# Decoder layer on one core: partition sums on TensorE, all queries in the fold stage, folded values beside the first softmax, another order of VectorE and GpSimd in the cross-attention

## The chip, the cores and the metric

One core of a Trainium2 chip runs the kernel. The metric is the device time of one execution in microseconds (us), the median of the runs. Engines are named as the profile names them: PE (TensorE matmul), PEld (its weight loads), DVE (VectorE), ACT (ScalarE), POOL (GpSimd), SP (SyncE, here only DMA issues). A tile is 128 rows of the 2048 x 256 activations; there are 16.

## The reference, cut to what matters

```python
x = x + self_attention(layernorm(x)) @ wo              # 16 heads of 16, causal by pages of 64
# cross-attention, one head of width 1024, 1601 keys, context c = ctx_1024
xn = layernorm(x)
e  = (xn @ Wq.T + bq) @ (c @ Wk.T + bk).T / sqrt(1024)
e  = where(mask == 0, -2**15, e)
x  = x + softmax(e) @ (c @ Wv.T + bv) @ Wo.T + bo
# feed: ternary weight, one scale for the whole tensor
xn = (x - mean(x)) * rsqrt(var(x) + 1e-3) * ln_gamma + ln_beta     # x is first layernormed too
beta = mean(abs(weight));  w_q = clip(round(weight / (beta + 1e-5)), -1, 1)
gamma = max(abs(xn))                                   # over all rows and columns
x = x + (clip(xn * 128 / gamma, ...) @ w_q) * (gamma * beta / 128)
```

Two of these lines sum or compare over all 128 partitions: `beta` and `gamma`.

## The kernel before

Four stages run one after the other, each in `nc.Block`s whose end all engines wait for.

`self_attention` (to 553.4 us of the span) isn't touched by the change. It leaves its result in the SBUF tile `attn`.

`fold` (553.4 to 620.5 us) does two things at once. It multiplies `attn` by `wo` and adds it to `x`, normalises the sum to `xn`, turns it with PE transposes and keeps it as `x2_t` (256 features on partitions, 2048 rows). And it folds the weights of the cross-attention: `w_qk` = Wq.T Wk, `w_vo` = Wv.T Wo, a bias `bias_c`, and the values of all 1601 keys with the output weight in them, `v_out`. PE takes its steps from the list `ORDER` (lines 889 to 892) written out by hand; ACT follows the same list. In it `turn` transposes four tiles of `attn` (first copied to `attn_s` by POOL, `stage`, line 913), `output` is the product with `wo`, `norm` transposes `xn`, and `job` n is one product of weights: 0 and 1 rows of bias, 2 and 3 `w_qk`, 4 and 5 `w_vo`, 6 the bias column (32 matmuls that are one column wide, lines 1065 to 1069), 7 to 13 `v_out` for two key tiles each. DVE runs `add` and `norm` for each block of four tiles and last computes the ternary feed weight; for its mean POOL sums `abs_sum` over the partitions (`partition_all_reduce`, line 937).

`cross` (620.7 to 882.3 us) goes over the 16 tiles in program order on every engine, as a loop of pairs of tiles (`pairs`, line 1189). PE's `body(i)` first runs `score(i + 1)`: it makes q~ of the next tile (8 matmuls of 128 columns, line 1353), waits until ACT has copied it with its bias (line 1314), and multiplies it with the 1601 context columns into four PSUM banks (line 1361). Then it transposes the softmax of tile i (line 1376) and multiplies it with `v_out` (line 1388). DVE's `body(i)` copies two of the four chunks of the transposes (line 1278), then `take(i + 1)`: masked copy out of PSUM (line 1264), row maximum (line 1266). ACT computes the exponential (line 1319). POOL fills `e` with the value of masked keys for the next tile (line 1223). After the product of tile i, DVE adds it to `x`, takes mean and variance (lines 1287 to 1296), waits for seven small steps of POOL that give the scale (lines 1229 to 1241), writes `z` (line 1299), waits for POOL's products with gamma and beta (lines 1245, 1247) and takes the row maximum (line 1302), all before it touches the chunks of tile i + 1. After the loop `x3` is transposed into `x3_t`.

`feed` (882.3 us to the end) reduces the 16 row maxima, has POOL take the maximum over partitions (line 1455), and then scales, clips, multiplies with the ternary weight and stores.

Of the kernel before, what the change touches and what calls it, by code (L numbers as in the profile page):

```python
# [17 lines left out]
I32 = mybir.dt.int32  # L18
# [6 lines left out]
P = 128  # L25
# [788 lines left out]
def fold(nc, ctx, io, keep, psum):  # L814
# [7 lines left out]
    def sem(name):  # L822
# [10 lines left out]
    w_vo = sb("w_vo", [P, EC, E])  # L833
# [4 lines left out]
    abs_all = sb("abs_all", [P, 1])  # L838
    limit = sb("limit", [P, 2])
    above = sb("above", [P, EC, E])  # L840
    attn_s = sb("attn_s", [P, TPB, E])
# [14 lines left out]
    w_bank = [banks(psum, 6), banks(psum, 7)]  # L856

# [3 lines left out]
    staged = sem("staged")  # L861
# [20 lines left out]
    abs_everywhere = sem("abs_everywhere")  # L882
    limit_done = sem("limit_done")
# [3 lines left out]
    V_FIRST = 7  # L887
# [6 lines left out]
    def v_tiles(n):  # L894
        return range(2 * (n - V_FIRST), min(2 * (n - V_FIRST) + 2, S2_TILES))

    def keys_of(j):
        return P if j < S2_TILES - 1 else S2_TAIL

    with nc.Block() as block:  # L900

        @block.sync
        def _(sp):
            sp.dma_start(b_o[:, :], bass.AP(io["bo"].tensor, 0, [[0, P], [1, E]])).then_inc(b_o_loaded, 16)
            sp.dma_start(ffn_w[:, :, :], io["ffn_w"].rearrange("(c p) e -> p c e", p=P)).then_inc(ffn_w_loaded, 16)

        @block.gpsimd
        def _(pool):
            nc.gpsimd.memset(eps[:, :], LN_EPS).then_inc(set_done, 1)
            nc.gpsimd.memset(minus_half[:, :], -0.5).then_inc(set_done, 1)  # L910
            pool.wait_ge(set_done, 2)

            def stage(tb):

                pool.wait_ge(a_ready, tb * EC)
                nc.gpsimd.tensor_copy(attn_s[:, :, :], attn[:, bass.ds(tb * TPB, TPB), :]).then_inc(staged, 1)
# [13 lines left out]
            stage(0)  # L930
            with pool.Fori(0, NB - 1) as tb:
                stage(tb + 1)
                norm(tb)
            norm(NB - 1)

            pool.wait_ge(abs_ready, 1)
            nc.gpsimd.partition_all_reduce(abs_all[:, :], abs_sum[:, :], P, ReduceOp.add).then_inc(abs_everywhere, 1)

        @block.vector
        def _(dve):  # L940
# [36 lines left out]

            dve.wait_ge(w_ready, 1)
# [8 lines left out]
            with dve.Fori(1, NB) as tb:  # L987
# [3 lines left out]
            dve.wait_ge(ffn_w_loaded, 16)  # L991
            nc.vector.tensor_reduce(abs_sum[:, :], ffn_w[:, :, :], axis=mybir.AxisListType.XY, op=ALU.add,
                                    apply_absolute_value=True).then_inc(abs_ready, 1)
            dve.wait_ge(abs_everywhere, 1)
            nc.vector.tensor_scalar(keep["beta"][:, :], abs_all[:, :], 1.0 / (E * E), None, ALU.mult).then_inc(limit_done, 1)
# [10 lines left out]
        def _(act):  # L1006
            def take(n):

                act.wait_ge(w_ready, n + 1)
                bank = w_bank[n % 2]  # L1010
                if n < V_FIRST:
                    dst = {2: w_qk[:, 0, :], 3: w_qk[:, 1, :], 4: w_vo[:, 0, :], 5: w_vo[:, 1, :],
                           6: bias_c[:, :]}[n]
                    last = nc.scalar.activation(dst, bank[:, 0:EC if n == 6 else E], ACT.Copy)
                else:
                    for m, j in enumerate(v_tiles(n)):
                        rows = keys_of(j)
                        last = nc.scalar.activation(v_out[0:rows, j, :], bank[0:rows, m * E:(m + 1) * E], ACT.Copy)
                last.then_inc(w_copied, 1)
# [8 lines left out]
            def turn_norm(tb):  # L1028
                for c in range(EC):
                    act.wait_ge(n_ready, tb * EC + c + 1)  # L1030
                    nc.scalar.activation(x2_t[:, c, tb, :], n_bank[c], ACT.Copy).then_inc(n_copied, 1)

            steps = {"turn": turn_attn, "norm": turn_norm, "job": lambda n: take(n) if n >= 2 else None,
                     "output": lambda tb: None}
# [4 lines left out]
        def _(pe):  # L1039
# [5 lines left out]
            def job(n):  # L1045
# [19 lines left out]
                elif n == 6:  # L1065
# [4 lines left out]
                else:  # L1070

                    pe.wait_ge(w_copied, 4)
                    for m, j in enumerate(v_tiles(n)):
                        rows = keys_of(j)
                        last = product(bank[0:rows, m * E:(m + 1) * E], lambda e: ctx_t[:, e, j * P:j * P + rows],
                                       lambda e: w_vo[:, e, :], EC)
                last.then_inc(w_ready, 1)

            def turn(tb):

                pe.wait_ge(staged, tb + 1)
                pe.wait_ge(a_copied, tb * EC)
                for c in range(EC):
                    for k in range(TPB):
                        last = nc.tensor.transpose(a_bank[c][:, k * P:(k + 1) * P], attn_s[:, k, c * P:(c + 1) * P],
                                                   ident[:, :])
# [13 lines left out]
            def normed(tb):  # L1100
                pe.wait_ge(xn_ready, tb * TPB + TPB)
                pe.wait_ge(n_copied, tb * EC)
# [6 lines left out]
            steps = {"turn": turn, "output": output, "norm": normed, "job": job}  # L1109
# [6 lines left out]
def cross(nc, ctx, io, keep, psum):  # L1116
# [7 lines left out]
    ctx_t, w_qk, bias_c, v_out = keep["ctx_t"], keep["w_qk"], keep["bias_c"], keep["v_out"]  # L1124
    x2_t, row_fill, x3, abs_max = keep["x2_t"], keep["row_fill"], keep["x3"], keep["abs_max"]
    x3_t = keep["x3_t"]
    mask = sb("mask", [P, 2, S2], I32)
# [7 lines left out]
    gamma = sb("gamma", [P, E])  # L1135
    beta = sb("beta_row", [P, E])
# [16 lines left out]
    q_bank = psum[:, 4 * BLK - E:4 * BLK]  # L1153
    t_bank = [banks(psum, n) for n in (4, 5, 7)]
    y_bank = banks(psum, 6)

    x_bank = [[banks(psum, n) for n in pair] for pair in ((0, 1), (2, 3), (4, 5), (0, 1))]

    mask_loaded = [sem(f"mask_loaded{n}") for n in range(2)]
# [455 lines left out]
```

## Time and profile before

| what | value |
|---|---|
| time, median of 3 runs | 914.88 us (911.33 to 915.14) |
| the profiled execution: its own time, its span | 913.99 us, 912.2 us |
| PE busy | 808.8 us, 89% of the span |
| DVE busy | 581.9 us, 64% |
| ACT busy | 413.7 us, 45% |
| POOL busy | 178.3 us, 20% |
| mean granted clock of TensorE | 0.933 of full |
| PE in `cross`, products with the context (L1361) | 256 records, 95.7 us |
| PE in `cross`, products with the values (L1388) | 416 records, 94.6 us |

The span runs from the first to the last instruction; the execution's own time has 1.8 us more around it. An fp32 matmul leaves two records in the trace, so 16 records of L1361 are the 8 matmuls of one tile. The clock has two levels, 2.4 GHz (1.00) and 1.2 GHz (0.50); a window's figure between them is a mix. Idle time is shown with what ended it, in brackets.

### The profile page before, as it was taken

To read this page: it belongs to the slowest core of one execution; us is meant where nothing else is said; L and a number is where in the kernel's file an instruction comes from. 1 tells how busy PE (TensorE), PEld (TensorE's weight loads), DVE (VectorE), ACT (ScalarE), POOL (GpSimd) and SP (SyncE) were. 2 spreads that over 40 slices of the span, in tenths; PEclk is the share of its full clock that TensorE was granted. 3 is DMA by queue.
4 is the path that set the end of the run, shared out by engine and by line. 5 is a ranking of instruction groups with operands and counts; after the bars stand their busy time and mean duration, and the time that the engine had idled before them with its cause. 6 is when DMAs were issued, how large, how long until landed. Compare 5 with 4: busy or idle time off the path is not lost. (4 is left out here: it accounts for less than half of the span.)

```text
span 912.2 us, 14049 instructions
## 1 busy us (share of the span) xinstructions
PE 808.8 (89%) x4252; PEld 406.5 (45%) x4252; DVE 581.9 (64%) x1047; ACT 413.7 (45%) x851; POOL 178.3 (20%) x263
## 2 busy tenths in 40 slices
PE   7865898999899999899999798895899999999847
PEld 5431232333223332223333226783576767667636
DVE  4998497889788899888886401772244535445414
ACT  1551553766467766567777692221222222222211
POOL 2662000000000000000000000433044453534410
PEclk9995897999899999989999898998899999999977
DMA  7794311200000000000700000002112112121002
GB/s 200 206 273 126 93 48 36 59 24 24 1 1 1 0 1 1 1 1 21 249 0 1 1 1 18 1 1 86 71 36 72 62 46 72 36 72 36 1 1 92
DMA packets 27084, 47.26 MB, mean 52 GB/s; under 512 B 6048, under 2 KB 22944, under 8 KB 26272
## 3 DMA queue, kind: packets, MB, share of 16 engines
q1 hardware_dynamic: 24096, 43.81, 15.8%
q10 hardware_dynamic: 2944, 2.89, 1.2%
q8 instruction: 25, 0.41, 0.2%
q14 instruction: 19, 0.16, 0.1%
HBM read 38.16 MB, written 8.39 MB: 51 GB/s over the span
## 5 line engine op out<-in xcount | busy, mean ns | idle before, releaser
L507 DVE TENSOR_REDUCE part_max<-psum 128x1 f32<-128x512 f32 (+3 forms) x560 | 344.2, 670 | 72.6 <-PE psum L706 68.0
L619 ACT ACTIVATE probs<-psum 128x512 f32<-128x512 f32 (+3 forms) x640 | 295.4, 539 | 170.8 <-PE psum L731 157.7
L706 PE MATMUL psum<-k_stack,q_stack 96*128 (+6 forms) x640 | 221.2, 374 | 17.9 <-DVE psum L493 11.5
L731 PE MATMUL psum<-q_stack,k_stack 98*128 98x512 bf16 (+6 forms) x640 | 209.2, 366 | 19.6 <-DMA q_stack<-shift 12.5
L746 PE MATMUL psum<-probs,v_group 128*17 128x512 f32 (+3 forms) x1280 | 151.0, 545 | 0.3
L706 PEld LDWEIGHTS psum<-k_stack,q_stack 96*128 (+3 forms) x640 | 61.1, 100 | 172.3 <-DVE part_max L507 81.5
L731 PEld LDWEIGHTS psum<-q_stack,k_stack 98*128 98x128 bf16 (+3 forms) x640 | 61.5, 100 | 109.9 <-issue 37.9
L1361 PE MATMUL psum<-q_stack,qc_t 128*128 128x512 f32 (+1 forms) x256 | 95.7, 528 | 12.8 <-ACT qc_t L1314 12.8
L407 POOL COPY v_group<-v_all 128x272 f32 (+1 forms) x40 | 16.8, 425 | 429.9 <-PE psum L746 429.9
L1388 PE MATMUL psum<-v_out,p_t 128*128 128x256 f32 (+1 forms) x416 | 94.6, 385 | 3.1 <-DVE p_t L1278 3.1
L1388 PEld LDWEIGHTS psum<-v_out,p_t 128*128 128x128 f32 (+1 forms) x416 | 79.0, 193 | 13.7 <-DVE p_t L1278 3.5
L1361 PEld LDWEIGHTS psum<-q_stack,qc_t 128*128 128x128 f32 x256 | 45.9, 194 | 63.5 <-issue 47.6
L1330 ACT ACTIVATE p_t<-psum 128x512 f32<-128x512 f32 x32 | 19.1, 598 | 103.1 <-PE psum L1376 103.1
L1319 ACT ACTIVATE e<-e,neg 128x1601 f32<-128x1601 f32 x16 | 26.1, 1632 | 79.3 <-DVE neg L1268 75.1
L746 PEld LDWEIGHTS psum<-probs,v_group 128*17 128x17 f32 x1280 | 21.5, 96 | 50.5 <-ACT probs L619 30.8
L1264 DVE COPY_PREDICATED e<-mask,psum 128x1601 f32<-128x1601 int32 x16 | 31.2, 1949 | 19.4 <-POOL e L1250 14.9
L1223 POOL TENSOR_TENSOR e<-zeros_s,row_fill 128x1601 f32<-128x1601 f32 x15 | 42.8, 2852 | 0.5 <-POOL e L1250 0.3
L1299 DVE TENSOR_SCALAR z<-x_sb,mv,scale 128x256 f32 (+1 forms) x16 | 6.6, 413 | 42.2 <-POOL scale L1241 42.2
L1278 DVE COPY p_t<-psum 128x512 f32<-128x512 f32 (+1 forms) x32 | 14.2, 484 | 29.0 <-PE psum L1376 29.0
L1266 DVE TENSOR_REDUCE neg<-e 128x1 f32<-128x1601 f32 x16 | 29.1, 1821 | 0.5
L530 DVE RECIPROCAL rsum<-psum 128x16 f32<-128x16 f32 x16 | 4.1, 254 | 37.7 <-PE psum L717 37.1
L1229 POOL TENSOR_TENSOR va<-mv,consts 128x1 f32<-128x1 f32 x16 | 3.0, 189 | 126.1 <-DVE mv L1296 126.1
(121 smaller groups left out, 708.4 us busy)
## 6 DMA issues: line engine op xcount, KB each, us to landing
mask<-in_mask SPq DMA_DIRECT2D x16, 800.5 KB, 4.4
pieces<-k_stack SPq DMA_DIRECT2D x24, 256.0 KB, 4.8
q_stack<-pieces SPq DMA_DIRECT2D x24, 256.0 KB, 4.3
k_stack<-pieces SPq DMA_DIRECT2D x24, 256.0 KB, 4.7
x_sb<-in_x SPq DMA_DIRECT2D x4, 512.0 KB, 8.7
out<-y SPq DMA_DIRECT2D x4, 512.0 KB, 2.9
q_stack<-in_ctxT SPq DMA_DIRECT2D x1, 1601.0 KB, 10.9
probs<-in_cos ACTq DMA_DIRECT2D x4, 256.0 KB
```

What stands on the lines that cost most here:

```text
L507: nc.vector.tensor_reduce(part_max[:, h:h + m, r, c:c + 1], src, axis=AX_X, op=ALU.max).then_inc(m_read, 1)
L619: nc.scalar.activation(probs[:, s % 2, h, col:BLK], s_bank[h][:, col:BLK], ACT.Exp, scale=ATTN_SCALE).then_inc(exp_done, 1)
L706: last = nc.tensor.matmul(out, q_stack[b][0:rows, g * G + h, r * P:(r + 1) * P], k_stack[c][0:rows, g * G + h, 0:keys], start=True, stop=True)
L731: nc.tensor.matmul(s_bank[h][:, col:BLK], k_stack[s // TPB][0:rows, g * G + h, (s % TPB) * P:(s % TPB + 1) * P], q_stack[b][0:rows, g * G ...
L746: last = nc.tensor.matmul(o_bank[32 * h:32 * h + VW, col:BLK], v_group[:, s, h, :], probs[:, s % 2, h, col:BLK], start=s == 0, stop=s == s ...
L1223: nc.gpsimd.tensor_tensor(e[:, 1 - h, :], zeros[:, :], row_fill[:, bass.ds(i + 1, 1)].to_broadcast([P, S2]), ALU.add).then_inc(filled, 1)
L1264: nc.vector.copy_predicated(e[:, h, :], mask[:, h, :], e_bank).then_inc(e_taken, 1)
L1266: nc.vector.tensor_reduce(neg[:, h:h + 1], e[:, h, :], axis=AX_X, op=ALU.max).then_inc(max_done, 1)
L1319: nc.scalar.activation(e[:, h, :], e[:, h, :], ACT.Exp, scale=X_SCALE, bias=neg[:, h:h + 1], accum_out=esum[:, h:h + 1]).then_inc(exp_done, 1)
L1330: nc.scalar.activation(p_t[:, j:j + m, :].rearrange("p j q -> p (j q)"), t_bank[n % 3][:, 0:m * P], ACT.Copy).then_inc(t_copied_a, 1)
L1361: last = nc.tensor.matmul(e_bank[:, c0:c1], qc_t[:, h, k, :], ctx_t[:, k, c0:c1], start=k == 0, stop=k == EC - 1)
L1388: mm = nc.tensor.matmul(y_bank[:, 0:E], p_t[0:keys, j, :], v_out[0:keys, j, :], start=j == 0, stop=j == S2_TILES - 1)
```

## The change

- `fold`, attention: `attn_s` and POOL's `stage` go; PE transposes `attn` itself.
- `fold`, queries: a step `("query", tb)` for each block of four tiles multiplies `x2_t` by `w_qk` (4 matmuls of 512 columns) and ACT writes the result with its bias back over `x2_t`. `score` in `cross` loses its 8 matmuls and the wait for ACT; ACT's `prepare` becomes one copy from SBUF, made two tiles ahead.
- `fold`, values: jobs 7 to 13 go. `cross` runs them as `V_JOBS` between `score(0)` and the first `body`, with ACT's copies before and after the first exponential.
- Partition sums: the sum of `abs_sum` is a matmul with a tile of ones (step `("sum", 0)`). In `feed` a PE transpose, a DVE maximum of one row and a matmul with ones take the place of POOL's instruction. DVE reduces the feed weight at the start of `fold`.
- Loads of gamma, beta and the first two mask tiles are issued in `fold` instead of at the start of `cross`.
- Order in `cross`: DVE's `z` and row maximum of tile i - 1 are done in `body(i)`, on both sides of `take(i + 1)`, instead of at the end of `body(i - 1)`. POOL does the fill of tile i + 1, then `finish(i - 1)`, then the seven steps of tile i (`measure`). The first pair of tiles is written out ahead of the loop.

```diff
-    JOBS = V_FIRST + -(-S2_TILES // 2)
     ORDER = [("turn", 0), ("job", 0), ("output", 0), ("job", 1), ("turn", 1), ("job", 2), ("output", 1),
              ("norm", 0), ("turn", 2), ("job", 3), ("output", 2), ("norm", 1), ("turn", 3), ("job", 4),
-             ("output", 3), ("norm", 2), ("job", 5), ("job", 6), ("job", 7), ("norm", 3)]
-    ORDER += [("job", n) for n in range(V_FIRST + 1, JOBS)]
+             ("output", 3), ("norm", 2), ("job", 5), ("job", 6), ("query", 0), ("query", 1), ("sum", 0),
+             ("query", 2), ("norm", 3), ("query", 3)]
...
+            def query(tb):
+
+                act.wait_ge(n_ready, in_n.index(("query", tb)) * EC + EC)
+                act.wait_ge(w_copied, 5)
+                for c in range(EC):
+                    nc.scalar.activation(x2_t[:, c, tb, :], n_bank[c], ACT.Identity,
+                                         bias=bias_c[:, c:c + 1]).then_inc(n_copied, 1)
...
+            def query(tb):
+
+                pe.wait_ge(n_copied, in_n.index(("query", tb)) * EC)
+                pe.wait_ge(w_copied, 2)
+                for c in range(EC):
+                    for k in range(EC):
+                        last = nc.tensor.matmul(n_bank[c], w_qk[:, k, c * P:(c + 1) * P], x2_t[:, k, tb, :],
+                                                start=k == 0, stop=k == EC - 1)
+                    last.then_inc(n_ready, 1)
...
+                nc.tensor.matmul(sum_at, ones[:, :], abs_sum[:, :], start=True, stop=True).then_inc(abs_everywhere, 1)
...
                 for n, (j, m) in enumerate(CHUNKS):
...
+                first = isinstance(i, int) and i == 0
+                if not first:
+                    scale_row(i - 1)
                 if not last:
                     take(i + 1, 1 - h)
+                if not first:
+                    largest(i - 1)
...
+            for n, tiles in enumerate(V_JOBS):
+                act.wait_ge(v_ready, n + 1)
+                for m, j in enumerate(tiles):
+                    rows = keys_of(j)
+                    last = nc.scalar.activation(v_out[0:rows, j, :], v_bank[n % 2][0:rows, m * E:(m + 1) * E], ACT.Copy)
+                last.then_inc(v_copied, 1)
+                if n == 1:
+                    exponential(0, 0)
...
             def score(i, h):
 
-                pe.wait_ge(qc_copied, i * EC)
                 pe.wait_ge(e_taken, i)
-                for c in range(EC):
-                    for k in range(EC):
-                        last = nc.tensor.matmul(q_bank[:, c * P:(c + 1) * P], w_qk[:, k, c * P:(c + 1) * P],
-                                                x2_t[:, k, :, :].rearrange("p b t -> p (b t)")[:, bass.ds(i * P, P)],
-                                                start=k == 0, stop=k == EC - 1)
-                last.then_inc(qc_ready, 1)
-                pe.wait_ge(qc_copied, (i + 1) * EC)
+                pe.wait_ge(qc_copied, i + 1)
...
             score(0, 0)
+            for n, tiles in enumerate(V_JOBS):
+
+                if n >= 2:
+                    pe.wait_ge(v_copied, n - 1)
...
+            pe.wait_ge(v_copied, len(V_JOBS))
             pairs(pe, body)
...
-            pool.wait_ge(top_done, 1)
-            nc.gpsimd.partition_all_reduce(top_all[:, :], top[:, :], P, ReduceOp.max).then_inc(top_everywhere, 1)
...
+            pe.wait_ge(top_done, 1)
+            nc.tensor.transpose(top_row, top[:, :], ident[:, :]).then_inc(top_turned, 1)
+            pe.wait_ge(top_found, 1)
+            nc.tensor.matmul(top_all, ones[0:1, :], top_1[:, :], start=True, stop=True).then_inc(top_everywhere, 1)
```

## Rows read from the trace of the kernel before

**Rows 1.** Windows: stretch, length, busy PE, PEld, DVE, ACT, POOL, PEclk, DMA, GB/s.

```profile
760.24:847.24 87.00, 82.71 (x379) 60.07 (x379) 40.84 (x67) 21.25 (x36) 37.82 (x60) 1.00 0.14 47
607.00:608.00 1.00, 1.00 (x4) 0.82 (x3) 0.26 (x1) 0.00 (x0) 0.71 (x1) 0.50 0.00 0
```

**Rows 2.** Timeline of one tile in `cross`: start, duration, engine, line, operation, idle before.

```profile
745.74 5.81 PE L1361 MATMUL psum<-q_stack,qc_t 128*128 128x512 f32 x16 [0.71 <-ACT qc_t L1314]
...
752.46 0.89 DVE L1278 COPY p_t<-psum 128x512 f32<-128x512 f32 x2 [1.23 <-PE psum L1376]
...
752.84 5.79 PE L1388 MATMUL psum<-v_out,p_t 128*128 128x256 f32 x26
...
753.66 1.95 DVE L1264 COPY_PREDICATED e<-mask,psum 128x1601 f32<-128x1601 int32 x1 [0.31 <-POOL e L1223]
...
757.68 1.63 ACT L1319 ACTIVATE e<-e,neg 128x1601 f32<-128x1601 f32 x1 [4.19 <-DVE neg L1268]
...
758.47 1.05 PE L1353 MATMUL psum<-x_t,w_qk 128*128 x8
...
760.24 4.99 PE L1361 MATMUL psum<-q_stack,qc_t 128*128 128x512 f32 x11 [0.71 <-ACT qc_t L1314]
...
762.76 0.19 POOL L1241 TENSOR_TENSOR scale<-ra,rb 128x1 f32<-128x1 f32 x1
```

**Rows 3.** Timeline of `fold`, 555 to 621 us.

```profile
555.71 1.97 PE L1085 MATMUL psum<-ident,attn_s 128*128 128x128 f32 x8 [2.46 <-POOL attn_s L916]
...
557.47 5.74 PE L1042 MATMUL psum<-q_stack 128*128 128x257 f32 x16
...
578.29 1.02 DVE L969 CUSTOM_DVE_ANT_0 dump<-xn,row_w 128x256 f32<-128x256 f32 x1
...
579.47 0.48 DVE L969 CUSTOM_DVE_ANT_0 dump<-xn,row_w 128x256 f32<-128x256 f32 x1
...
590.35 1.09 PE L1085 MATMUL psum<-ident,attn_s 128*128 128x128 f32 x8 [2.38 <-POOL attn_s L916]
...
598.19 1.04 PE L1105 MATMUL psum<-ident,xn 128*128 128x128 f32 x8
...
599.07 7.09 PE L1042 MATMUL psum<-q_stack 128*128 128x256 f32 x48
...
606.02 3.66 PE L1042 MATMUL psum<-w_vo,q_stack 128*128 128x256 f32 x8
...
610.26 1.10 ACT L1031 ACTIVATE x_t<-psum 128x512 f32<-128x512 f32 x2
...
620.09 0.38 ACT L1018 ACTIVATE v_out<-psum 65x256 f32<-65x256 f32 x1 [0.20 <-PE psum L1042]
```

**Rows 4.** Timeline of the start of `cross`.

```profile
622.77 5.81 PE L1361 MATMUL psum<-q_stack,qc_t 128*128 128x512 f32 x16 [0.71 <-ACT qc_t L1314]
...
632.23 2.84 POOL L1250 TENSOR_TENSOR e<-zeros_s,row_fill 128x1601 f32<-128x1601 f32 x1 [9.95 <-issue]
...
639.21 1.63 ACT L1319 ACTIVATE e<-e,neg 128x1601 f32<-128x1601 f32 x1 [16.49 <-DVE neg L1268]
...
641.50 8.55 PE L1361 MATMUL psum<-q_stack,qc_t 128*128 128x512 f32 x16 [2.04 <-ACT qc_t L1314]
```

**Rows 5.** Timeline of the last tile and of the start of `feed`.

```profile
867.53 5.84 PE L1388 MATMUL psum<-v_out,p_t 128*128 128x256 f32 x18 [3.09 <-DVE p_t L1278]
...
882.58 0.17 DVE L1459 TENSOR_REDUCE top<-abs_max 128x1 f32<-128x16 f32 x1 [2.52 <-PEq L1197]
888.50 0.38 POOL L1455 PARTITION_ALL_REDUCE top_all<-top  x1 [8.88 <-issue]
888.91 0.16 DVE L1462 RECIPROCAL to_q<-top_all 128x1 f32<-128x1 f32 x1 [6.16 <-POOL top_all L1455]
```

**Rows 6.** Timeline of a small PE transpose between two DVE operations in self-attention.

```profile
515.05 0.22 DVE L512 TENSOR_REDUCE neg_max<-part_max 128x16 f32<-128x64 f32 x1
...
515.72 0.28 DVE L518 CAST shift<-psum 16x128 bf16<-16x128 f32 x1 [0.45 <-PE psum L712]
```

More of the change, by code:

```diff
@@ L905, in _ @@
             sp.dma_start(ffn_w[:, :, :], io["ffn_w"].rearrange("(c p) e -> p c e", p=P)).then_inc(ffn_w_loaded, 16)
+            masks = io["mask"].rearrange("(t p) s -> t p s", p=P)
+            for name in ("gamma", "beta"):
+                sp.dma_start(keep[name + "_row"][:, :], bass.AP(io[name].tensor, 0, [[0, P], [1, E]]))\
+                    .then_inc(keep["rows_loaded"], 16)
+            for h in range(2):
+                sp.dma_start(keep["mask"][:, h, :], masks[h]).then_inc(keep["mask_loaded"][h], 16)
         @block.gpsimd
@@ L1010, in take @@
                 bank = w_bank[n % 2]
[L1011 to L1018, printed above, removed]
+                dst = {2: w_qk[:, 0, :], 3: w_qk[:, 1, :], 4: w_vo[:, 0, :], 5: w_vo[:, 1, :], 6: bias_c[:, :]}[n]
+                last = nc.scalar.activation(dst, bank[:, 0:EC if n == 6 else E], ACT.Copy)
                 last.then_inc(w_copied, 1)
@@ L1029, in turn_norm @@
                 for c in range(EC):
[L1030 removed]
+                    act.wait_ge(n_ready, in_n.index(("norm", tb)) * EC + c + 1)
                     nc.scalar.activation(x2_t[:, c, tb, :], n_bank[c], ACT.Copy).then_inc(n_copied, 1)
[L1033 to L1034 removed]
+            def query(tb):
[4 more added lines that the diff above has]
+                                         bias=bias_c[:, c:c + 1]).then_inc(n_copied, 1)
+            steps = {"turn": turn_attn, "norm": turn_norm, "query": query,
+                     "job": lambda n: take(n) if n >= 2 else None,
+                     "output": lambda tb: None, "sum": lambda n: None}
             for what, n in ORDER:
@@ L1187, in cross, with keys_of, pairs @@
     PAIRS = TILES // 2
-    def pairs(engine, body, first=None):
-        with engine.Fori(0, PAIRS - 1) as k:
+    def keys_of(j):
+        return P if j < S2_TILES - 1 else S2_TAIL
+    def pairs(engine, body):
+        for h in range(2):
+            body(h, h, False)
+        with engine.Fori(1, PAIRS - 1) as k:
             for h in range(2):
@@ L1335, in body @@
                     exponential(i + 1, 1 - h)
-            prepare(0, 0)
-            exponential(0, 0)
+            for h in range(2):
+                src = queries[:, :, 0, h * P:(h + 1) * P]
+                nc.scalar.activation(qc_t[:, h, :, :], src, ACT.Copy).then_inc(qc_copied, 1)
+            for n, tiles in enumerate(V_JOBS):
[6 more added lines that the diff above has]
+                    exponential(0, 0)
             pairs(act, body)
@@ L1392, in _ @@
             score(0, 0)
+            for n, tiles in enumerate(V_JOBS):
+                if n >= 2:
+                    pe.wait_ge(v_copied, n - 1)
+                for m, j in enumerate(tiles):
+                    for k in range(EC):
+                        last = nc.tensor.matmul(v_bank[n % 2][0:keys_of(j), m * E:(m + 1) * E],
+                                                ctx_t[:, k, j * P:j * P + keys_of(j)], w_vo[:, k, :],
+                                                start=k == 0, stop=k == EC - 1)
+                last.then_inc(v_ready, 1)
+            pe.wait_ge(v_copied, len(V_JOBS))
             pairs(pe, body)
@@ L1544, in build @@
             keep["w_qk"] = sbo("w_qk", [P, EC, E])
+            keep["w_vo"] = sbo("w_vo", [P, EC, E])
+            keep["ones"] = sbo("ones", [P, P])
+            keep["mask"] = sbo("mask", [P, 2, S2], I32)
+            keep["gamma_row"] = sbo("gamma_row", [P, E])
+            keep["beta_row"] = sbo("beta_row", [P, E])
+            keep["mask_loaded"] = [own.enter_context(nc.semaphore(f"mask_loaded{n}")) for n in range(2)]
+            keep["rows_loaded"] = own.enter_context(nc.semaphore("rows_loaded"))
             keep["bias_c"] = sbo("bias_c", [P, EC])
```

146 lines of the change are left out of this document (73 added, 73 removed).

## The prediction

> **What bounds the kernel now.** I read the busy time by windows first. Over six tiles of `cross` PE is busy for 82.71 of 87.00 us at the full clock, DVE for 40.84 and POOL for 37.82 [rows 1]: PE sets the pace and the others have half their time free. The timeline of one tile then shows where PE's other time is. A tile lasts 14.50 us (760.24 - 745.74). It is the product with the context (5.64 us to the first transpose, 5.81 with its tail), the transposes (1.46), the product with the values (5.63 to the next step), q~ of the next tile (1.05) and a wait of 0.71 for ACT's copy of q~ [rows 2]. So 1.05 + 0.72 = 1.77 us of each tile are q~ and its round trip. Third, the timeline of `fold`: DVE's norm chain sets the time up to the last block, and then PE's seven value jobs run to its end at 620.47 us [rows 3]. Fourth, the start and the end of `cross`, where PE stands still: 13 us between the first and the second product with the context, the second then at half the clock [rows 4], 3.09 us in the last tile, and the wait for POOL's maximum over partitions [rows 5].
>
> **q~ out of the loop.** `score` 2 to 15 each lose 1.77 us, if nothing else ends later than PE: 14 x 1.77 = **-24.8 us**. What is late next? Counted from the start of a product with the context, DVE's chunk copies end at +7.6 us (752.46 + 0.89 - 745.74). Then comes `z` of the tile before, moved there, which is half the size of one of the two copies that take 0.89, so 0.45 at most; 0.31 of idle stand in that place now. The masked copy then ends at about +10.1, where it ended at +9.87 (753.66 + 1.95 - 745.74). The banks are needed at +12.73, so 2.6 us are free. The exponential, which starts 4.02 us after the masked copy and takes 1.63, ends near +13.9 with its read-out, and the transposes that want it start at 12.73 + 5.64 = +18.4: 4.5 us free [rows 2]. ACT's copy of q~ is made two tiles ahead and waits for nothing late. POOL's scale of the tile before ends 4.5 us after the product with the values (762.95 - 758.47). The fill of 2.84 follows at once and ends near +7.4, before DVE's +8.1 [rows 2, 4]; that is the narrowest of these margins, and missing it by 1 us still costs PE nothing, because of the 2.6. Behind DVE's wait for the scale in `scale_row` stands `take`; behind POOL's wait for `z` in `finish` stand the seven steps, whose input comes only at the end of the tile. New period 12.73 us.
>
> **Queries in `fold`.** Four steps of 4 x 512 = 2048 columns. The 3202 columns of a product with the context take 5.64 us [rows 2], so a query takes 5.64 x 2048 / 3202 = 3.6 us. ACT copies both halves only after both are made (1.10 us by the copies of the same shape [rows 3], 1.3 with the two hand-overs), and the next query waits for that. The list runs: `norm` 2, jobs 5 and 6, query 0, 1, 2, `norm` 3, query 3. Before, the transposes of `norm` 2 start at 598.19 and job 6 ends at 606.06 [rows 3]. Two things shift this. First, PE needn't wait 2.46 us for POOL's copy of `attn`: it can start about 1.1 us earlier, as soon as the stage begins, but 1.97 us for 8 transposes and 5.74 us for job 0 (7.09 for three times the records later) are at the half clock, while later 8 transposes take 1.09 [rows 3]. Some of the gain is given back, as the clock rises no earlier for it: -0.6, bounds 0 and -3. Second, without POOL's copies one of DVE's four dot products per block takes 0.48 instead of 1.02 us [rows 3]: 2 x 0.54 = -1.1, bounds 0 and -1.1. So job 6 ends at 604.3. Query 0 is then at risk: the 3.66 us of the value job right behind job 6 cover 8 records, and the clock was 0.50 although PE was busy the whole time [rows 1, 3]. Job 6 is 32 matmuls of one column. Half that cost, +0.9, is in the sum; its bounds are 0 and +3.6. Then 3 x (3.6 + 1.3) = 14.7, the transposes and their copy 1.8, and 3.6 + 1.3 = 4.9. End of `fold`: 604.3 + 0.9 + 14.7 + 1.8 + 4.9 = 626.6, against 620.47: **+6.1 us**. The end is now a chain of hand-overs between PE and ACT; nothing covers it.
>
> **Values in the first tile.** ACT needs 0.4 us for the first copy of q~ (0.38 for 256 columns at 620.09 [rows 3]), so the first product with the context starts about 0.8 us after the stage's end and ends at +6.5. POOL's fill follows its memsets: it no longer waits 9.95 us [rows 4], since the loads are issued 70 us earlier and no `partition_all_reduce` stands before it, and ends near +5.3. From the masked copy to the end of the exponential are 4.02 + 1.63 us and 0.2 of read-out [rows 2]: done near +12.5. Meanwhile PE does 26 matmuls of 256 columns, 2 x 5.63 = 11.3 us by the product with the values [rows 2]. Every second job's bank is free in time, since the exponential holds ACT for 1.8 us only, and with the last copy the first `body` begins at +18.1. That is 626.6 + 18.1 = 644.7. The second product with the context started at 641.50 before, but took 8.55 us at the half clock against 5.81 [rows 4]; now PE was busy just before. Ends: 650.4 against 649.9, so **+0.5 us** in all to this point, the +6.1 included. The cover works both ways: 13 us of standing still take up the value jobs and the longer `fold`.
>
> **Last tile.** DVE no longer stands in the chain of `z` and POOL's products when the last transposes are ready. The product with the values keeps neither its wait of 3.09 us nor the half clock behind it: 5.84 us for 18 records, where 26 take 5.79 [rows 2, 5]. That is 3.09 + 5.84 - 18/26 x 5.79 = 4.9 us. The exponential is about 0.2 later: **-4.7 us**. The norm of tile 15 behind it is the same chain as before.
>
> **Maximum over partitions.** From the end of DVE's `top` (882.75) to `to_q` (888.91) are 6.16 us, of which POOL's instruction is 0.38 [rows 5]. Instead: PE transpose, DVE maximum, PE matmul. A DVE to PE to DVE trip takes 0.45 us [rows 6]; twice that and 0.2 for the maximum are 1.1. **-5.1 us**, bounds -3 (the trips at twice the price and more) and -5.3. The Trainium skill speaks against this edit: "GPSIMD Engine Reference", section "Engine selection", names GpSimd for reductions over partitions. The same page, "Instruction dispatch", says that the first call of freshly loaded code pays about 6 us. By the first rule alone POOL should keep the maximum and the sum would have no such term; the row sides with the second: 5.66 us without work in front of 0.38. In `fold` the sum over partitions had cover and has it now: 0.
>
> **Nothing** for the moved loads (SP issues two before them as before, and no one waits for the masks until 70 us later), the DVE reduction at the head of `fold` (512 columns, while DVE waits for the 5.74 us of job 0 [rows 3]), and the written-out first pair.
>
> **Sum.** -24.8 + 0.5 - 4.7 - 5.1 = -34.1 us. Against the profiled execution: 913.99 - 34.1 = 879.9. That run stands 0.9 below the median of 914.88, well inside the spread; I take 880.
>
> **Rivals.** (1) *PE no longer sets the pace.* DVE's `z` and POOL's fill fall on each other, or another wait takes the place of the 0.72. Then 14 x 0.72 = 10 come back: 890. For: the fill has 0.7 us of margin. Against: the banks have 2.6 us behind it. (2) *The queries run at the half clock throughout*: 4 x 3.6 more, 894. For: a drop stands behind job 6 [rows 1], and bursts of 3.6 us with gaps of 1.3 us follow. Against: after a gap of 2.38 us in `fold` 8 transposes take 1.09 us, at the full clock [rows 3]. The skill's "TensorE: Matmul & The Clock Gate", section on oscillation, describes such a loss from short gaps between groups of matmuls, and would have it in every query. (3) *POOL's wait at the start of `cross` stays* (the profile names nothing that ended it, so it may be code loading that comes anyway). With 6 us of it left, the exponential and the ACT copies behind it come 5 us later: 885. (4) *Slower than before*: in `cross` the clock falls to half and stays there, since PE has no other limit now. A tile is then 12.73 us longer, and from 34.1 / 12.73 = 2.7 such tiles on the change loses; with four it is 931. For: the half clock follows every standstill in rows 4 and 5. Against: 87 us at 1.00 with less PE work per time. (5) *Better*: the clock stays up at the start of `fold` and behind job 6 and rises sooner in `feed`: -6, so 874. (6) *The removal doesn't remove*: POOL's share of the 6.16 us was hidden. Excluded, as DVE waits for it by name [rows 5].
>
> **How the numbers follow.** Forecast 0.65, (1) 0.10, (2) 0.06, (3) 0.07, (4) 0.03, (5) 0.09. The forecast's own bounds: the start of `fold` -3, query clock -0.9 to +2.7, trips +2: 875 to 885. The range 872 to 890 takes in (1), (3) and (5) and leaves out (2), (4) and tails. A measurement of this kernel can tell about 0.5% (4.6 us) from no change. Only (4) is slower, and nothing likely lies within 0.5%: faster 0.96, same 0.01, slower 0.03.
>
> **What would show it.** The products with the context start 12.7 us apart. `fold` ends near 626 and its four queries are 4.9 us apart. The second product with the context takes 5.8 us. The last product with the values has no wait in its middle. `top` to `to_q` takes about 1.3 us. It is wrong if the period is above 13 us, or if half-clock windows stand in `cross` after its first tile.

## The result

| | before | changed |
|---|---|---|
| time, median | 913.22 us (4 runs) | 876.18 us (875.08 to 882.21, 4 runs) |
| ratio, 95% interval | | 0.9607 (0.9563 to 0.9651) |
| profiled execution: its own time, span | 913.99, 912.2 us | 882.21, 880.4 us |

By the ratio the time falls by 36 us; forecast was 880 us with a range of 872 to 890. Timed again beside three variants (control, below) the changed kernel had 877.55 us, ratio 0.9623 (0.9599 to 0.9648). The profiled execution is the longest of its runs. To see why, and to compare experiments closer than their times allow, I cut each trace at six marks: the first POOL memset of `fold`, that of `cross`, the first transpose of the softmax, the last addition to `x`, `top`, `to_q`. This table is worked out from the timelines of one execution each:

```
us             before fold  fold  first tile  other tiles  x3  top to to_q  rest   span
before              554.4   66.3     29.1       223.6      9.1     6.3      23.3   912.2
changed             556.4   72.1     25.4       192.5      9.1     1.6      23.3   880.4
control             554.3   72.1     23.8       192.5      9.1     1.6      23.8   877.0
feed_only           557.5   66.4     29.2       223.6      9.1     1.6      23.9   911.2
order_only          552.9   66.3     29.1       218.8      8.3     6.4      22.6   904.2
q_in_loop           551.7   58.0     30.3       218.8      8.2     1.6      23.5   892.1
v_in_fold           552.9   80.7     15.9       192.5      9.0     1.6      22.4   875.1
stage_back          553.0   75.7     23.8       192.5      9.1     1.6      23.7   879.3
reduce_back         553.9   72.0     31.6       192.5      8.2     1.6      23.6   883.5
mixed_jobs          554.3   72.1     23.8       192.5      9.1     1.6      23.8   877.0
more_banks          551.1   66.3     23.8       192.5      9.1     1.6      23.3   867.6
more_banks_again    554.0   66.3     23.8       192.5      8.2     1.6      23.6   870.0
both                551.2   64.6     25.5       192.5      9.0     1.6      23.2   867.7
split               549.2   72.7     15.1       192.5      8.7     1.6      22.8   862.6
```

("control" is the changed kernel once more; the other names are those of the experiments below.) The self-attention ahead of `fold` is the same code in all of them and lasts 549.2 to 557.5 us. That is nearly all of the scatter between these executions. The later stages of the same code repeat to 0.1 us except where the clock differs: "x3" is 9.1 or 8.2 us long and "rest" varies by 1.4, with the place of the half clock that starts in "x3" in every trace. The profiled changed execution has 2.0 us more in self-attention than that of before. The stages from `fold` on are 33.8 us shorter: +5.7 in `fold`, -3.7 in the first tile, -31.1 in the others, -4.7 at the maximum.

**The profile after.** Two lines of the page, the costliest PE groups of `cross` (line, engine, operation, count, busy time, mean, idle before):

```profile
L1385 PE MATMUL psum<-q_stack,qc_t 128*128 128x512 f32 (+1 forms) x256 | 93.2, 517 | 2.6 <-ACT qc_t L1361 2.1
...
L1412 PE MATMUL psum<-v_out,p_t 128*128 128x256 f32 (+1 forms) x416 | 92.7, 380 | 0.0
```

The idle time before the products with the context is 2.6 us, where it was 12.8, all of it spent on ACT's copy of q~ (page of before, the same group on line 1361). A tile of the changed kernel (start, duration, engine, line, operation), to be held against [rows 2]; of the last group only the part before the end of the window is counted:

```profile
686.34 5.71 PE L1385 MATMUL psum<-q_stack,qc_t 128*128 128x512 f32 x16
...
690.64 0.19 POOL L1235 TENSOR_TENSOR scale<-ra,rb 128x1 f32<-128x1 f32 x1
690.78 2.85 POOL L1253 TENSOR_TENSOR e<-zeros_s,row_fill 128x1601 f32<-128x1601 f32 x1
...
693.77 0.40 DVE L1287 TENSOR_SCALAR z<-x_sb,mv,scale 128x256 f32 x1
694.09 1.96 DVE L1276 COPY_PREDICATED e<-mask,psum 128x1601 f32<-128x1601 int32 x1
...
698.13 1.63 ACT L1341 ACTIVATE e<-e,neg 128x1601 f32<-128x1601 f32 x1 [4.13 <-DVE neg L1280]
...
698.97 1.45 PE L1385 MATMUL psum<-q_stack,qc_t 128*128 128x512 f32 x3
```

PE starts the next product with the context after 12.63 us, with no wait in front. The masked copy ends 9.71 us after the tile's start (forecast 10.1) and POOL's fill at +7.29 (forecast 7.4), 0.46 before the masked copy that needs it begins, where the forecast had 0.7.

`fold` and the first tile, against [rows 3, 4]:

```profile
556.42 1.06 PE L1068 MATMUL psum<-ident,attn 128*128 128x128 f32 x8 [1.20 <-PEq L285]
...
557.32 3.64 PE L1033 MATMUL psum<-q_stack 128*128 128x257 f32 x16
...
603.43 6.38 PE L1098 MATMUL psum<-x_t,w_qk 128*128 128x512 f32 x8
...
611.16 3.70 PE L1098 MATMUL psum<-x_t,w_qk 128*128 128x512 f32 x8 [1.36 <-ACT x_t L1020]
...
629.01 7.48 PE L1385 MATMUL psum<-q_stack,qc_t 128*128 128x512 f32 x16 [2.15 <-ACT qc_t L1361]
...
636.33 11.44 PE L1423 MATMUL psum<-w_vo,q_stack 128*128 128x256 f32 x52
636.74 1.96 DVE L1276 COPY_PREDICATED e<-mask,psum 128x1601 f32<-128x1601 int32 x1 [19.67 <-PE psum L1385]
...
648.24 5.81 PE L1385 MATMUL psum<-q_stack,qc_t 128*128 128x512 f32 x16 [0.47 <-ACT v_out L1366]
```

Three things in it: the stage begins at the full clock (1.06 us for the 8 transposes that took 1.97), the first query takes 6.38 us where the others take 3.70, and the first product with the context takes 7.48 where the next takes 5.81. Job 6 stands right before the first query. It is 16 matmuls of one column (8 for each of two columns), which leave 32 records; the text on the kernel before and the prediction count the records as matmuls. The clock in the windows over job 6 and the first query (stretch, length, busy PE, PEld, DVE, ACT, POOL, PEclk, DMA share, GB/s):

```profile
602.00:603.50 1.50, 1.50 (x10) 1.50 (x9) 0.89 (x6) 0.00 (x0) 0.27 (x2) 0.51 0.00 0
603.50:609.80 6.30, 6.30 (x9) 2.37 (x8) 4.88 (x11) 0.17 (x1) 3.29 (x2) 0.57 0.00 0
609.80:611.20 1.40, 0.04 (x2) 0.04 (x1) 0.40 (x3) 1.27 (x2) 0.00 (x0) 1.00 0.00 0
```

The last tile and the maximum, against [rows 5]:

```profile
838.96 1.73 PE L1400 MATMUL psum<-ident,e 128*128 128x128 f32 x13 [0.87 <-ACT e L1341]
...
840.52 5.79 PE L1412 MATMUL psum<-v_out,p_t 128*128 128x256 f32 x26
...
855.49 0.17 DVE L1493 TENSOR_REDUCE top<-abs_max 128x1 f32<-128x16 f32 x1 [2.52 <-PEq L1202]
...
855.72 0.37 PE L1542 MATMUL psum<-ident,top 128*1 128x128 f32 x1 [1.17 <-DVE top L1493]
856.12 0.28 DVE L1496 TENSOR_REDUCE top<-psum 1x1 f32<-1x128 f32 x1 [0.46 <-PE psum L1542]
...
857.08 0.17 DVE L1498 RECIPROCAL to_q<-psum 128x1 f32<-128x1 f32 x1 [0.67 <-PE psum L1544]
```

### The profile page after: what moved, and what is told of

Its sections match the earlier page's. It is cut to its first block and busy times, and to the rows that moved or that the text cites. A ratio compares the mean times of both kernels' runs of the same rounds, so it can differ in the third digit from the quotient of the medians.

```text
span 880.4 us, 13756 instructions
## 1 busy us (share of the span) xinstructions
PE 800.3 (91%) x4161; PEld 393.1 (45%) x4161; DVE 577.9 (66%) x1048; ACT 413.2 (47%) x843; POOL 173.5 (20%) x258
## 5 line engine op out<-in xcount | busy, mean ns | idle before, releaser
L706 PE MATMUL psum<-k_stack,q_stack 96*128 (+6 forms) x640 | 218.5, 369 | 18.6 <-DVE psum L493 11.2
L1385 PE MATMUL psum<-q_stack,qc_t 128*128 128x512 f32 (+1 forms) x256 | 93.2, 517 | 2.6 <-ACT qc_t L1361 2.1
L1412 PE MATMUL psum<-v_out,p_t 128*128 128x256 f32 (+1 forms) x416 | 92.7, 380 | 0.0
L1400 PE MATMUL psum<-ident,e 128*128 128x128 f32 (+1 forms) x208 | 26.2, 276 | 0.9 <-ACT e L1341 0.9
L1033 PE MATMUL psum<-q_stack 128*128 128x256 f32 (+2 forms) x128 | 25.9, 351 | 0.0
```

Of the source, the lines that this page charges most:

```text
L706: last = nc.tensor.matmul(out, q_stack[b][0:rows, g * G + h, r * P:(r + 1) * P], k_stack[c][0:rows, g * G + h, 0:keys], start=True, stop=True)
L1385: last = nc.tensor.matmul(e_bank[:, c0:c1], qc_t[:, h, k, :], ctx_t[:, k, c0:c1], start=k == 0, stop=k == EC - 1)
L1400: last_t = nc.tensor.transpose(t_bank[n % 3][0:keys, (j - j0) * P:(j - j0 + 1) * P], e[:, h, j * P:j * P + keys], ident[:, :])
L1412: mm = nc.tensor.matmul(y_bank[:, 0:E], p_t[0:keys, j, :], v_out[0:keys, j, :], start=j == 0, stop=j == S2_TILES - 1)
```

## The experiments

Theory at the start: PE's path sets the time, and the parts add as in the prediction's sum. The first two experiments add one part to the kernel before, the next four take one back from the changed kernel, and the others alter the changed kernel further.

### The maximum alone, on the kernel before

```diff
-            nc.gpsimd.partition_all_reduce(top_all[:, :], top[:, :], P, ReduceOp.max).then_inc(top_everywhere, 1)
+            nc.tensor.transpose(top_row, top[:, :], ident[:, :]).then_inc(top_turned, 1)
+            nc.tensor.matmul(top_all, ones[0:1, :], top_1[:, :], start=True, stop=True).then_inc(top_everywhere, 1)
```

> The kernel before with one part alone: the maximum over partitions in feed by PE transpose, DVE and PE matmul, and the tile of ones it needs. Theory: the 6.33 us from the start of top to to_q become 1.6 as in the changed kernel, so 4.7 us less than before (ratio 0.995), and nothing else moves; POOL's other partition sum stays and still costs its wait at the start of cross. Rival: part of the gain of the changed kernel's end comes from its other order, and this alone gives under 2 us.

Measured (feed_only): 907.93 us, ratio 0.9956 (0.9939 to 0.9972), 4.0 us less; from `top` to `to_q` 1.59 us instead of 6.33, and no other stage from `fold` to "x3" moves by more than 0.1. As the theory had it.

### The order of DVE and POOL alone, on the kernel before

```diff
+                if not first:
+                    scale_row(i - 1)
                 if not last:
                     take(i + 1, 1 - h)
+                if not first:
+                    largest(i - 1)
```

> The kernel before with one part alone: z and the row maximum of the tile before on both sides of take, POOL's fill ahead of finish and of the seven steps, first pair written out. Theory: PE sets the pace, so the 14.50 us of a tile stay (the next product with the context still waits 0.71 for the copy of q~), and only the last tile gains, where the product with the values loses its wait of 3.09 us and the half clock behind it: 5.3 us less than before (ratio 0.994). Rival: the order alone shortens every tile, period under 14.3 us and over 8 us less; or DVE's z in front of take delays the masked copy and the period rises.

Measured (order_only): 906.32 us, ratio 0.9942 (0.9918 to 0.9967), 5.3 us less. The timeline of PE:

```profile
729.66 5.81 PE L1385 MATMUL psum<-q_stack,qc_t 128*128 128x512 f32 x16 [0.71 <-ACT qc_t L1338]
...
744.16 5.81 PE L1385 MATMUL psum<-q_stack,qc_t 128*128 128x512 f32 x16 [0.72 <-ACT qc_t L1338]
```

The period is 14.50 us as before, with the same 0.7 of wait, and the table shows 4.8 us less in "other tiles". The order alone pays at the last tile only. What it is worth together with q~ out of the loop isn't shown: every kernel with q~ out of the loop has the new order as well.

### q~ in the loop again

```diff
-             ("query", 2), ("norm", 3), ("query", 3)]
+             ("norm", 3)]
...
+                        last = nc.tensor.matmul(q_bank[:, c * P:(c + 1) * P], w_qk[:, k, c * P:(c + 1) * P],
```

> The changed kernel with one part undone: q~ of each tile is made in the loop again, and fold has no queries. Theory (both sides are on PE's path): fold ends about 20 us earlier (near its 52nd us instead of its 72nd), cross gets 14 x 1.84 = 25.8 us for the tiles and about 3.7 for the first two, so 9 us more than the changed kernel, about 885. Rival 1: the queries in fold cost nothing net and the whole 26 us come back: about 902. Rival 2: the queries' move is worth nothing, fold's cost eats it: 876.

Measured (q_in_loop): 894.49 us, ratio 0.9808 (0.9777 to 0.9839), 18 us above the changed kernel and so halfway between the theory (885) and the first rival (902). The tiles behave as expected (+26.3 us), and the first one has 4.8 more. But `fold` is only 14.1 shorter, not 20:

```profile
608.75 0.69 DVE L991 TENSOR_TENSOR w_tern<-above,ffn_w 128x512 f32<-128x512 f32 x1
...
609.91 2.05 PE L1386 MATMUL psum<-x_t,w_qk 128*128 128x128 f32 x8 [5.00 <-PEq L892]
```

Without queries DVE's chain ends the stage, with the last norm and the ternary weight. The changed kernel's queries run in part beside that chain, and so moving q~ is worth 17 us by the marks (26.3 + 4.8 - 14.1), more than I expected here. The 4.8 are taken from the profiled changed execution, whose first product was at the half clock; against the control it is 6.5.

### The value jobs in `fold` again

```diff
+    ORDER += [("value", n) for n in range(7)]
...
-            for n, tiles in enumerate(V_JOBS):
```

> The changed kernel with one part undone: the seven value jobs stand at the end of fold again, behind the last query. The prediction counted them as free beside the first softmax, so it expects 9.7 to 11 us more, 886. Rival, from the trace of the changed kernel: with POOL's long wait gone, PE would only stand still for the masked copy (about 2.2 us) between the first two products with the context; fold ends 10.5 us later, the second product starts 9.8 us sooner after the first, and the first runs at the full clock (1.7 less): no difference, 875.

Measured (v_in_fold): 877.73 us, ratio 0.9628 (0.9596 to 0.966), against 0.9607 and 0.9623 for the changed kernel: no difference. Its second product with the context:

```profile
634.22 5.78 PE L1405 MATMUL psum<-q_stack,qc_t 128*128 128x512 f32 x16 [1.26 <-ACT qc_t L1388]
...
640.24 1.93 DVE L1303 COPY_PREDICATED e<-mask,psum 128x1601 f32<-128x1601 int32 x1 [28.32 <-PE psum L1405]
...
642.23 7.50 PE L1405 MATMUL psum<-q_stack,qc_t 128*128 128x512 f32 x16 [2.23 <-DVE e L1303]
```

PE waits 2.23 us for the masked copy and nothing else. `fold` is 8.7 us longer, the first tile 7.8 to 9.5 shorter, although the second product is at the half clock here (7.50 us instead of 5.8, granted clock 0.50 from 643.6 to 646.9). The move that I counted as covered gains nothing: of the 13 us of standing still in [rows 4] 2.2 are left without any job to fill them. Most of the rest was POOL's late first fill and goes with it.

### POOL's copy of `attn` again

```diff
+                pe.wait_ge(staged, tb + 1)
-                                                   attn[:, tb * TPB + k, c * P:(c + 1) * P], ident[:, :])
+                                                   attn_s[:, k, c * P:(c + 1) * P], ident[:, :])
```

> The changed kernel with one part undone: POOL copies four tiles of attn to attn_s before PE transposes them. The prediction gave its removal 0.6 us at the start of fold and 1.1 in DVE's dot products: 1.7 us more, 878. Rival, from the trace of the changed kernel: what counts is the clock, which stays at 1.00 at the start of fold when PE doesn't wait there; with the wait back the first 6 us run at the half clock and the queries start 5.3 us later: 881.

Measured (stage_back): 880.47 us, ratio 0.9655 (0.9625 to 0.9684), 3 to 4 us more. The intervals of the two kernels overlap, so the table decides: against the control `fold` is 3.6 us longer and no other stage up to "x3" moves.

```profile
554.29 1.97 PE L1079 MATMUL psum<-ident,attn_s 128*128 128x128 f32 x8 [2.47 <-POOL attn_s L917]
...
556.05 5.74 PE L1043 MATMUL psum<-q_stack 128*128 128x257 f32 x16
```

With the wait of 2.47 us the first steps are at the half clock, as in [rows 3]. In all four traces with POOL's copy the transposes take 1.97 us and job 0 takes 5.63 to 5.74. In the ten without it the transposes take 1.06 to 1.79 us and job 0 3.64 (changed, v_in_fold) to 5.06 (q_in_loop). So the half clock is shortened, by 1 to 3 us in the two together; by how much differs between executions. The 3.6 us lie between the 1.7 of the prediction and the 5.3 of the rival, which was read from the profiled changed execution, all of whose start is at the full clock.

### The sum over partitions by POOL again

```diff
+            nc.gpsimd.partition_all_reduce(abs_all[:, :], abs_sum[:, :], P, ReduceOp.add).then_inc(abs_everywhere, 1)
...
-             ("output", 3), ("norm", 2), ("job", 5), ("job", 6), ("query", 0), ("query", 1), ("sum", 0),
+             ("output", 3), ("norm", 2), ("job", 5), ("job", 6), ("query", 0), ("query", 1),
```

> The changed kernel with one part undone: the sum of abs_sum over partitions by POOL, at the end of its work in fold. If POOL's wait of 9.95 us at the start of cross came from that instruction, it comes back although all loads have landed long before: at least 6 us of idle without a releaser in front of the first fill, masked copy and exponential later, the value jobs behind the exponential's ACT too: 3 to 6 us more than the changed kernel, 879 to 882. Rival: the wait was for the loads of gamma and beta, which are still early here: no wait, 876.

Measured (reduce_back): 885.51 us, ratio 0.9708 (0.9659 to 0.9758), 8 to 9 us more, where 3 to 6 were expected. Of the last group only the part before the end of the window is counted.

```profile
634.78 2.84 POOL L1265 TENSOR_TENSOR e<-zeros_s,row_fill 128x1601 f32<-128x1601 f32 x1 [7.33 <-issue]
...
637.76 1.96 DVE L1280 COPY_PREDICATED e<-mask,psum 128x1601 f32<-128x1601 int32 x1 [22.21 <-POOL e L1265]
...
641.79 1.63 ACT L1345 ACTIVATE e<-e,neg 128x1601 f32<-128x1601 f32 x1 [5.31 <-DVE neg L1284]
...
644.10 6.25 PE L1427 MATMUL psum<-w_vo,q_stack 128*128 128x256 f32 x15 [4.87 <-ACT v_out L1370]
```

All loads landed some 60 us earlier, and still POOL's first arithmetic stands 7.33 us behind the memsets, with no releaser. Masked copy, exponential and ACT's copies of the values follow late, and PE, which waited for nothing there, now waits 4.87 us between the value jobs. Behind that wait the granted clock is 0.50 from 642.8 to 649.6 us, and the 20 records of value jobs there take 7.33 us, about 2.9 more than at the pace of the changed kernel (11.44 us for 52; an estimate from these two). So the first tile takes 31.6 us instead of 23.8. The expectation had the wait and not the clock. The Trainium skill, "GPSIMD Engine Reference", "Instruction dispatch", gives about 6 us for the first call of freshly loaded code. It tells that of the loaded kernel; these traces show it in front of the reduction (5.66 us in `feed`) and again in front of the ordinary instruction that follows it. The lines of that ordinary instruction, POOL's first fill, show what the timeline of the engine leaves out; first before, then reduce_back, then the changed kernel (line, engine, operation, count, shortest, median and longest in ns, first and last start):

```profile
L1250 POOLq MODIFY_POOL_CONFIG  x2: 11/11/11, 622.3 to 622.3; - x2
...
L1265 POOLq MODIFY_POOL_CONFIG  x2: 11/11/11, 627.5 to 627.5; - x2
L1265 POOL TENSOR_TENSOR e<-zeros_s,row_fill x1: 2842/2842/2842, 634.8 to 634.8; 128x1601 f32<-128x1601 f32 x1
...
L1261 POOL TENSOR_TENSOR e<-zeros_s,row_fill x1: 2852/2852/2852, 630.1 to 630.1; 128x1601 f32<-128x1601 f32 x1
```

POOL's queue has a pair of `MODIFY_POOL_CONFIG` records in front of every `partition_all_reduce` (5.4 to 5.8 us ahead of it) and in front of the first fill behind it. All four kernels with the sum on POOL (before, feed_only, order_only, reduce_back) have the pair on that fill; the ten others have none anywhere after the first 2 us. The 9.95 us of the kernel before had a second part: the row of beta landed only at 625.8, and the fill started 6.4 us after that. So some 2.6 us of them (9.95 - 7.33, an estimate) go with the early loads; no run moves the loads alone.

### One-column matmuls mixed between wide ones

```diff
+                    for c, n in narrow[2 * e:2 * e + 2]:
+                        nc.tensor.matmul(w_bank[0][:, c:c + 1], cw_k[:, n, c * P:(c + 1) * P], cw_q[:, n, E:E + 1],
+                                         start=n == 0, stop=n == HC - 1)
+                    last = nc.tensor.matmul(w_bank[1][:, 0:E], cw_v[:, e, P:2 * P], cw_o[e],
+                                            start=e == 0, stop=e == HC - 1)
```

> The changed kernel with one change: the 32 matmuls of one column of job 6 are issued between the 8 wide ones of job 5, two after each. Theory: the run of 3.4 us of one-column matmuls is what lets the clock fall before the first query (6.38 us instead of 3.70); mixed, it stays at 1.00 there and the kernel is 2.7 us faster, 873.5. Rival: the clock falls there anyway, for another reason: 876.

Measured (mixed_jobs): 877.64 us, ratio 0.9621 (0.9597 to 0.9645): no gain.

```profile
602.38 3.59 PE L1113 MATMUL psum<-x_t,w_qk 128*128 128x512 f32 x8
...
619.33 5.40 PE L1113 MATMUL psum<-x_t,w_qk 128*128 128x512 f32 x8 [0.74 <-ACT x_t L1013]
```

The edit puts two one-column matmuls before each wide one, not after it. The first query is at the full clock, so job 6 as a block did cause the fall there: the clock falls in the last 1.6 us of the block or within 0.3 us behind it in all eleven traces that have the block, and in none of the three that mix it. But now the fourth query takes 5.40 us. A later fall, behind hand-overs and transposes, takes over, and `fold` stays at 72.1 us. Why it comes there and not in the changed kernel isn't shown.

### Banks of their own for the queries

```diff
-                        last = nc.tensor.matmul(n_bank[c], w_qk[:, k, c * P:(c + 1) * P], x2_t[:, k, tb, :],
+                        last = nc.tensor.matmul((a_bank, y_bank)[tb % 2][c], w_qk[:, k, c * P:(c + 1) * P],
+                                                x2_t[:, k, tb, :], start=k == 0, stop=k == EC - 1)
```

> The changed kernel with one change: the queries write to four PSUM banks that the attention output no longer needs, two by turns, and norm 3 stands after query 1. PE then doesn't wait for ACT between the queries. Theory: the hand-overs are on the path (1.36 + 1.24 + 1.45 + 0.74 us of idle before the steps, and the transposes between), so fold ends about 6 us earlier and the kernel with it, 870. Rival: the time comes back as another wait, since norm 3 of DVE or the clock holds the end: under 2 us.

Measured (more_banks): 873.11 us, ratio 0.9585 (0.956 to 0.9611): 2 to 4 us less than the changed kernel, which wasn't timed beside it, though `fold` is 5.7 us shorter. So the two were timed once more, on one chip:

> The changed kernel itself, for the comparison with the three beside it. Both theories: fold 72 us long, first tile (start of cross to the first transposes) 23.8 or 25.4 with the half clock, 192.5 from there to the last x, and a ratio near 0.961.

> The queries in banks of their own once more, beside the changed kernel on one chip. In its trace fold is 66.3 us long instead of 72.1, but the times of the two differ by 3 us in the medians of different chips' runs. Theory: the 5.7 us are real and the rest is the length of self-attention, which the first look shows to differ by up to 6 us between executions of the same code: 5 to 6 us less than the control. Rival: they come back elsewhere, under 3 us less.

Measured (control, more_banks_again): 877.55 us, ratio 0.9623 (0.9599 to 0.9648), and 871.30 us, ratio 0.9557 (0.9536 to 0.9578). That is 6.3 us on one chip; the hand-overs were on the path, and the rest was scatter. The edit has two parts, the banks and `norm` 3 one place earlier, which weren't tried apart. The queries in the second trace:

```profile
602.00 8.81 PE L1105 MATMUL psum<-x_t,w_qk 128*128 128x512 f32 x16
...
611.69 7.03 PE L1105 MATMUL psum<-x_t,w_qk 128*128 128x512 f32 x16
```

Queries now run in pairs without a gap: 7.03 us for two, 8.81 where the first meets the half clock.

### Both, and the value jobs split

```diff
+    ORDER += [("value", n) for n in range(5)]
...
-    V_JOBS = [range(j, min(j + 2, S2_TILES)) for j in range(0, S2_TILES, 2)]
+    V_JOBS = [range(j, min(j + 2, S2_TILES)) for j in range(10, S2_TILES, 2)]
```

> Banks of their own and the one-column matmuls mixed in between job 5's. Theory A: the run of one-column matmuls is what costs the first query 1.8 to 2.8 us, and without hand-overs no other standstill follows: fold 64.5 us, 7 us less than the control. Theory B (mixed_jobs alone had its half clock in the fourth query instead of the first): the fall only moves, fold 66.3, 5.5 less.

> As the one before, with five of the seven value jobs back at the end of fold and two left between the first two products with the context. Theory: beside the first softmax PE has only the masked copy of 2.2 us to wait for, which two jobs of 1.7 us cover; in fold the five cover the last hand-over. Fold 8 us longer, first tile 8.3 shorter, 0 to 1.5 us less than the one before. Rival (more cover is better, all seven belong beside the softmax): 2 us or more slower than the one before.

Measured (both, split): 868.71 us, ratio 0.9533 (0.9506 to 0.9561), and 866.65 us, ratio 0.9516 (0.9496 to 0.9536). By the marks, both saves 1.7 us in `fold` and loses them to the half clock in the first tile (64.6 + 25.5 against 66.3 + 23.8); whether it beats the banks alone stays open. split takes 2.3 us off fold and first tile together (72.7 + 15.1). Of these 1.7 are the half clock of the first product, which doesn't come back: from 553 to 836 us its granted clock is 1.00 throughout. It is the only one of the versions without a fall in `fold` behind the start or in the tiles, and the fastest, 10.9 us below the changed kernel on the same chip.

## Why the prediction was right, point by point

- **q~ out of the loop**: -24.8 predicted. The tiles lose 26.3 us (192.5 against the 218.8 of order_only and q_in_loop). A tile lasts 12.62 to 12.69 us, where 12.73 was forecast. Mechanism as told; the fill's margin in front of the masked copy is 0.46 us, not 0.7, since DVE gets there 0.35 earlier and the fill only 0.1. It still decides nothing, because the banks have 2.9 us.
- **Queries in `fold`**: +6.1 predicted, +5.7 measured, out of two errors that cancel. Counted from the stage's start, `norm` 2 comes 5.3 us sooner (594.88 - 556.38 against 598.19 - 554.41) and 3.6 sooner in the control, not 1.7. The term that was mis-sized is "-0.6, bounds 0 and -3", the start of the stage: the first transposes of `xn` come 4.2 us sooner in the profiled execution, outside the bounds, and 2.5 in the control, and in stage_back they are back where they were (23.34 us from the start, 23.32 before). The term of -1.1 for the dot products holds: 0.54 and 0.53. Against the gain stand 2.8 us for the half clock in query 0 (0.9 in the sum), 0.7 for the end of job 6 at the same clock, and queries 5.05 us apart instead of 4.9. That the total came out is luck.
- **Values in the first tile**: +0.5 predicted for everything up to the second product; by the marks +2.0 in the profiled execution, whose first product is at the half clock, and +0.3 in the control, whose isn't. The total came out, but the step "13 us of standing still take up the value jobs" was wrong as a cause: the change itself ends the standing still, and v_in_fold shows that moving the jobs is worth nothing.
- **The sum in `fold`: 0** holds in `fold` itself (72.0 us in reduce_back, 72.1 in the control), but read as the price of POOL's sum it misleads: that price, 7.9 us by the marks, stands in the first tile. The prediction let POOL's 9.95 us go there for two causes at once, the early loads and the sum, and priced neither. reduce_back has the early loads and still gets 7.33 of them back. Rival 3, which kept this wait, named the right cause, but the change removes it: no `MODIFY_POOL_CONFIG` stands on the first fill any more.
- **Last tile**: -4.7 predicted, -4.8 measured (order_only).
- **Maximum**: -5.1 predicted, -4.7 measured. The small DVE, PE and DVE steps take 1.42 us from the end of `top`, where two trips of 0.45 and a reduction of 0.2 were reckoned.
- **Rivals**: PE still sets the pace (1); the clock fell for one query, not four (2), as the full-clock queries with gaps of 1.3 us in front show; none of tiles 1 to 15 is at the half clock (4). The sign "half-clock windows in `cross` after its first tile" did come, but behind the last tile: the granted clock is 0.50 from 851.3 to 855.4 us, in the transposes of `x3`, as it was there before the change (879.2 to 882.5). Rival 5 came in part: the profiled execution stays at the full clock at the start of `fold`, the control falls to half after 0.4 us there.

The sum from `fold` on is -33.8 in the profiled execution and -35.1 in the control, against -34.1 forecast.

## What to carry to other kernels

Cut the trace at the stages' starts before comparing executions: here one unchanged stage scatters by 8 us, while the others repeat to 0.1 where the clock is the same. When a wait "for nothing" stands in a profile, look at what the engine ran last, not only at what it waits for; a POOL reduction of 0.4 us cost 6 us in front and 7 behind, and only the records of POOL's queue on the waiting line told of it. And before work is moved into idle time, ask whether the change itself removes the cause of that idle time.

## What the runs showed of the hardware

- Behind `partition_all_reduce`, POOL's memsets ran at once, but its next arithmetic stood 7.33 us with every input ready (reduce_back), behind a pair of `MODIFY_POOL_CONFIG` records. Without the reduction the same instruction followed the memsets directly, and the pair was missing.
- In the changed kernel PE counted as busy for all of 602.0 to 603.5 us with one-column matmuls, behind 2.8 us more of them, and the granted clock was 0.51 there, half. The same matmuls mixed with wide ones (mixed_jobs, both, split) kept the full clock.
- Such a fall cost a query or a product 1.7 to 2.7 us. Removing the one in query 0 brought one in query 3 (mixed_jobs) or in the first product with the context (both); in split there was none.
